# Last layer of a four-layer graph network: the weighted sum's ten matmuls put in one piece ahead of the next tile's scores

## The reference

```python
def _L3_gnn_ref(x, batch, ei, W):
    src, dest = (ei[0], ei[1])
    qkv = x @ W
    q, k, v = jnp.split(qkv, [Fqk, 2 * Fqk], axis=-1)
    q = (q * scaling).reshape(n, H, Fh)
    k = k.reshape(n, H, Fh)
    v = v.reshape(n, H, Fhv)
    aw = jnp.einsum('ehf,ehf->eh', q[src], k[dest])
    m = jax.ops.segment_max(aw, src, num_segments=n)
    e = jnp.exp(aw - m[src])
    denom = jax.ops.segment_sum(e, src, num_segments=n)
    alpha = e / denom[src]
    out = jax.ops.segment_sum(alpha[:, :, None] * v[dest], src, num_segments=n)
    return out.reshape(n, Fv)
```

## Time and profile before

| | us |
|---|---|
| median of 3 runs | 1241.31 (1241.21 to 1241.64) |
| the profiled execution | 1241.29 |
| its span | 1239.6 |
| from the span to the time | 1.7 |

### The profile page before, as it was taken

How to read it: one execution, slowest core, us unless ns; L and a number is a source line. 1 busy time by engine, 2 the same in 40 slices (tenths; PEclk the granted TensorE clock), 3 DMA queues, 4 the chain that set the end, 5 groups by cost and what they waited for, 6 DMA issues and landing times. The chain is left out here.

```text
span 1239.6 us, 16221 instructions
## 1 busy us (share of the span) xinstructions
PE 1131.6 (91%) x5959; PEld 713.1 (58%) x5959; DVE 911.9 (74%) x1652; ACT 716.3 (58%) x901; POOL 63.5 (5%) x117
## 2 busy tenths in 40 slices
PE   4999899988989968889999999979969999999996
PEld 4666655547765543344455444446537777777775
DVE  5999970118558686979988997944438888888885
ACT  1324774016548664168788776744137777777774
POOL 3000032000002000000000000000000000000000
PEclk9999999999999968979999999979979999999999
DMA  4000000021030001103111100000021001111002
GB/s 156 5 1 1 1 2 1 1 70 66 1 79 17 1 0 49 61 1 146 45 45 45 45 24 3 0 1 1 1 52 27 18 10 27 27 27 27 2 1 83
DMA packets 24771, 36.18 MB, mean 29 GB/s; under 512 B 11874, under 2 KB 13204, under 8 KB 24694
## 3 DMA queue, kind: packets, MB, share of 16 engines
q1 hardware_dynamic: 24694, 35.14, 9.4%
HBM read 26.03 MB, written 2.70 MB: 23 GB/s over the span
## 5 line engine op out<-in xcount | busy, mean ns | idle before, releaser
L62 PE MATMUL wide<-arena 125*125 125x512 bf16 (+5 forms) x2076 | 463.0, 372 | 21.2 <-ACT arena L543 6.5
L62 PEld LDWEIGHTS wide<-arena 125*125 125x125 bf16 (+5 forms) x2076 | 253.1, 131 | 204.6 <-issue 88.9
L1756 PE MATMUL wide<-arena 125*65 125x512 f32 (+1 forms) x480 | 181.3, 514 | 0.0
L1367 PE MATMUL wide<-ident,arena 125*125 125x125 f32 (+3 forms) x954 | 131.6, 285 | 12.2 <-ACT arena L619 4.2
L751 ACT ACTIVATE arena<-arena,b 125x1250 f32<-125x1250 f32 x80 | 106.7, 1336 | 59.1 <-PE wide L1756 54.9
L1266 DVE TENSOR_TENSOR arena<-wide,arena 125x1250 f32<-125x1250 f32 x80 | 116.7, 1459 | 29.7 <-PE wide L1746 29.5
L1367 PEld LDWEIGHTS wide<-ident,arena 125*125 125x125 f32 (+3 forms) x954 | 116.6, 187 | 22.6 <-issue 10.3
L830 ACT ACTIVATE arena<-wide 125x1000 f16<-125x1000 f32 x80 | 80.7, 1009 | 80.8 <-PE wide L1367 80.8
L1756 PEld LDWEIGHTS wide<-arena 125*65 125x65 f32 x480 | 63.1, 138 | 101.0 <-issue 94.6
L1328 DVE SCALAR_TENSOR_TENSOR arena<-wide,arena 125x1000 f16<-125x1000 f32 x80 | 95.9, 1198 | 33.9 <-ACT arena L830 33.9
L845 ACT ACTIVATE arena<-arena,neg_max,unit 125x1250 f32<-125x1250 f32 x80 | 114.3, 1429 | 10.6 <-DVE neg_max L1355 10.6
(11 more groups left out here) (255 smaller groups left out, 1222.4 us busy)
## 6 DMA issues: line engine op xcount, KB each, us to landing
arena<-rows_kept SPq DMA_DIRECT2D x16, 625.0 KB, 5.5
arena<-arena SPq DMA_DIRECT2D x40, 156.2 KB, 2.9
arena<-in_L_gnn_W SPq DMA_DIRECT2D x3, 1024.0 KB, 8.2
x_nm<-in_x SPq DMA_DIRECT2D x2, 1250.0 KB
out<-x_nm SPq DMA_DIRECT2D x1, 2187.5 KB
arena<-in_L_gnn_W_l SPq DMA_DIRECT2D x1, 1024.0 KB, 6.4
arena<-in_L_gnn_W_r SPq DMA_DIRECT2D x1, 1024.0 KB, 9.1
arena<-in_L_gnn_Wk SPq DMA_DIRECT2D x1, 1024.0 KB, 5.4
```

The costliest lines, as they stand in the source:

```text
L62: mm = pe.matmul(ps[0:rows, lo:hi], lhsT, rhs[:, lo:hi], start=start, stop=stop, skip_group_check=True)
L1367: return pe.transpose(dst, src, ident[0:k, 0:k])
L1756: m = pe.matmul(psW[1][0:VA, lo:hi], v_gat[0:ROWS, t, h, :], ring[n % RINGS][0:ROWS, lo:hi], start=(t == 0), stop=(t == TILES - 1))
```

## The change

One call of `weigh_pair` in place of two in TensorE's loop. All five blocks of a step (ten matmuls) are put ahead of `score(n + 1)`; before, three blocks (six matmuls) stood ahead of it and two blocks (four matmuls) behind it.

```diff
                     half = n % 2
                     if 4 <= n < H * TILES + 4:
-                        weigh_pair((n - 4) // 2, (range(5 * half, 5 * half + 3)))
+                        weigh_pair((n - 4) // 2, range(5 * half, 5 * half + 5))
                     if n + 1 < H * TILES:
                         score(n + 1)
-                    if 4 <= n < H * TILES + 4:
-                        weigh_pair((n - 4) // 2, (range(5 * half + 3, 5 * half + 5)))
                     if n >= 6 and n % 2 == 0:
                         fold_pair((n - 6) // 2)
```

## The result

The changed kernel takes 1248.2 us (median of 5 runs, 1246.85 to 1248.66), the kernel before in the same comparison 1241.21 (1240.36 to 1241.64): a ratio of 1.0058 with a 95% interval of 1.0046 to 1.0070. It is slower, by 7.0 us, where 5.4 were forecast. The forecast's upper end, 1248.3, is a ratio of 1.0056. The two medians alone would give the same 1.0056; by the ratio of all executions, 1.0058, the result lies just above the range, closer to its end than the interval can tell.

The account below looks back on a forecast made before the run. TensorE was nearly full, but the path ran through VectorE's reduce and `add_quad` to the next transposes. Late reduce 3.1, fold 1.9 and odd steps 0.4 made 5.4 us on 1241.3: 1246.7 us, range 1243.0 to 1248.3.

Parts of the forecast that it names:

- The path through `add_quad`: From B's transposes through the reduce, `add_quad` and L1328 to D's transposes: 7.81 us, set by when the reduce can start.
- B: Even step with transposes at 1053.40 us, 3.90 us long; L1328 idles 0.39 us in it, waiting for ScalarE.
- D: Even step with transposes at 1061.21 us, 3.93 us long, forecast 4.03; its transposes' load waits 0.45 us, 18 times.
- The reduce late by 0.17 us: VectorE's reduce ahead of `add_quad` starts 0.17 us later because scores come 0.44 us later; 18 times, 3.1 us.
- A: Odd step with transposes at 1065.14 us, TensorE without idle time, 3.55 us long, forecast 3.57.
- The 0.05 us for a second wait: Allowance for a second wait on VectorE's semaphore instruction; makes the late reduce 18 times 0.22 at the range's upper end.
- The fold behind the scores, 0.10 us in 19 steps: In even steps without an `add_quad` behind them, the fold's matmuls take 0.10 us more behind scores; 1.9 us in all.
- Odd steps, 0.02 us more: Transposes directly behind the scores of odd steps cost net 0.02 us, 19 times, 0.4 us.
- The cover of 0.39 us in the other steps: L1328's idleness waiting for ScalarE, 0.39 us in B and 0.76 in A, hides a late reduce at no cost.
- rival 2: Scores become the path in every step, 0.17 us in 75 steps, 12.8 us: 1254 us; chance 0.05.
- What would show it: Timeline signs: idle time ahead of L1352 of 0.1 to 0.2 us, B to D 7.98 us, D's wait less deep.
- rival 1: Scores still arrive in time, reduce late by 0.03 us or less, not slower: 1241.3 to 1243.7 us; chance 0.16.

Follow-up runs that it names:

- four_one: Four blocks ahead of the scores and one behind in every step, against the kernel before: 1241.44 us against 1241.11, ratio 1.0003.
- even_only: All five blocks ahead of the scores in even steps alone, odd steps as in the kernel before: 1246.56 us, ratio 1.0049.
- fold_ahead: Changed kernel with the fold of even steps also ahead of the scores: 1254.07 us against 1241.33 for the kernel before, ratio 1.0102.
- fold_first: Kernel before with the two later blocks put behind the fold, scores unmoved: 1242.64 us against 1241.11, ratio 1.0012.
- odd_only: All five blocks ahead of the scores in odd steps alone, even steps as in the kernel before: 1242.47 us, ratio 1.0012.

## Why the prediction came out as it did

- *The path through `add_quad`.* Right. It is where B to D grew, 18 times, and the wait of the transposes is still counted 18 times. four_one, even_only and fold_ahead place the threshold and the slope.
- *The reduce late by 0.17 us.* This is the step that failed, in its size: the mechanism was right, but it is 0.27 us between B and D, of which 0.26 are the reduce. Two parts were mis-sized. The latency from the scores' end to the reduce was 0.22 us, not 0.19, which gives the 0.20 of even_only, as 0.44 + 0.22 - 0.46. And B's transposes, themselves behind scores, reach the weighted sum 0.06 us later. I had priced that only as the 0.03 us by which L830 is later, and booked it in A, not on the way of the scores to the reduce. 18 times 0.27 is 4.9 us where the prediction had 3.1. These 1.8 us are the whole miss of 1.6 and a little more: the fold and the odd steps came out 0.2 and 0.7 below the forecast, and 0.2 in the loop's first steps and 0.5 ahead of the loop were not in it. That the miss is no larger is in part luck, since these cancel. The 0.05 us for a second wait, from which the range's upper end was made, stand in no row; what the runs show in their place is the 0.03 us of latency and the 0.06 of the transposes.
- *The fold behind the scores, 0.10 us in 19 steps.* Right: D went from 3.93 to 4.02, and fold_first shows it alone. 1.7 us where 1.9 stood.
- *Odd steps, 0.02 us more.* Wrong in sign: A went from 3.55 to 3.53, some -0.3 us in all where +0.4 stood. So the loop's 6.5 is 4.9 + 1.7 - 0.3 and some 0.2 of the first steps.
- *What lies outside the loop.* I had nothing there. The profiled execution has 0.5 us ahead of the loop, well within the 3.0 us by which the start of the first transposes differs between the ten runs.
- *The cover of 0.39 us in the other steps.* Right: odd_only costs 1.4 us, L1328 still idles 0.21 us in B (ahead of 1058.76), and rival 2, all steps on the path, did not come. (Rival 2 was priced at 0.17 us a step, though its own condition asks for more than 0.39.)
- *What would show it.* B to D came out at 8.08 where 7.98 stood, D at 4.02 where 4.03 stood. The wait of D's transposes did not get less deep but grew by 0.13 us (0.36 to 0.49), since B to D grew by more than B itself. I expected the profile to mark idle time ahead of L1352, and it marks none at a gap of 0.11 us. By that sign alone I would have read rival 1. The starts themselves, and the reduce's 1.46 us in place of 1.45, are the sign.
- *The two rules of the Trainium skill.* The Trainium skill (Perfetto Trace Analysis, section Per-instruction lifecycle) calls TensorE's ends an estimate. The distance from that estimate to the reduce was 0.22 us at full clock and 0.19 at half, so the 0.19 was no fault of the half clock, and as a price it was 0.03 us too low. The other rule of the Trainium skill (TensorEngine Tiling (Array Packing), section Key Properties), that a change of the tiling mode drains TensorE, fits the idle 0.27 us of the load behind each group of scores, which is there in both orders. By its count alone the joins would have cost nothing more, and they did; a drain counted is not a drain priced, since what stands behind it paid from next to nothing (half precision weights of the weighted sum) to 0.09 us (fold).

## What to carry to other kernels

An engine at 98% of a stretch can still be waiting for another one every few steps, and an order that keeps its own work unchanged can make that wait longer: look for the step in which the other engine has no idle time, and measure how much room the transfer between them has there. Here it was 0.24 us, so two matmuls could be moved for nothing and four could not. When a step is made lighter, ask next what hung on the part that was put off: the output's store took back 3.5 us, about half of the gain, until the quad it waits for was left in place. And where a cost is some tenths of a us in a repeated step, compare the repeated stretch itself: here the two halves of the change added up to the whole within 0.03 us by the loop's stretch, and within 0.2 us by the times.

## What the runs showed of the hardware

- A weight load directly behind the 64-row scores started only after 0.27 us of idleness, whatever group it belonged to. Single precision groups then took longer: the fold's four matmuls 0.65 us in place of 0.55, the ten transposes 1.19 to the next group in place of 1.13. The weighted sum's four half precision matmuls took 0.44 us to the next group there, the same as the share of four in the middle of a group (1.09 us for ten less 0.65 for six).
- From the modelled end of a matmul to the start of a VectorE instruction that had waited for it, with one semaphore instruction of VectorE in between, it was 0.22 us at the 2.4 GHz level, and 0.24 us were enough to hide it altogether (four_one).
